# Early-fusion megakernel: last layernorm in token rows, softmax row sums on GpSimd, new order on every engine

## The reference, cut to what matters

```
h = concat(tokens(x) * pos, txt)
h = h + retention(layernorm(h))                  # A: 8 heads, complex, per-head norm, gate
u = layernorm(h)
q, k, v = u @ Wq + bq, u @ Wk + bk, u @ Wv + bv  # B: 8 heads of 16
attn = softmax(q k^T / 4)                        # rows of 97
o = (attn @ v) @ Wo + bo
t = layernorm(u + o) * ln1_g + ln1_b             # C
probs = softmax(t @ gate_W + gate_b)
out = h + expert[argmax](t) * max(probs)         # gelu((t @ W1) + b1) @ W2 + b2
```

## Time and profile before

| | |
|---|---|
| median of 3 runs | 1401.92 us (1400.88 to 1402.66) |
| the profiled execution, its own time | 1397.03 us |
| its span | 1395.2 us |
| PE busy, share of the span | 1346.4 us, 96% |
| DVE busy | 1008.2 us, 72% |
| ACT busy | 718.4 us, 51% |
| POOL busy | 407.4 us, 29% |
| mean granted TensorE clock | 0.993 |
| chain that ended last, share of PE | 90% |

### The profile page before, as it was taken

One profiled execution on the slowest core, in us unless ns is written; L12 is line 12 of the kernel. 1 busy time (PEld: TensorE's weight loads), 2 busy tenths in 40 slices (PEclk: granted clock), 3 DMA queues, 4 the chain that ended last, 5 costly groups with the idle time before them and its releaser, 6 DMA issues.

```text
span 1395.2 us, 40349 instructions
## 1 busy us (share of the span) xinstructions
PE 1346.4 (96%) x14878; PEld 988.3 (71%) x14879; DVE 1008.2 (72%) x2331; ACT 718.4 (51%) x1630; POOL 407.4 (29%) x268
## 2 busy tenths in 40 slices
PE   7899999999999999999999999999999986999998
PEld 5566666666666666666666666666666554999998
DVE  2677777777777777777777777777777865666665
ACT  2255555555555555555555555555555554556555
POOL 0002222222222222222222222222222225655666
PEclk9999999999999999999999999999999998999999
DMA  9422322232222222322222222232331002343332
GB/s 388 141 73 77 84 85 84 84 84 85 84 85 84 85 85 84 85 83 84 85 80 78 78 83 84 85 85 85 85 85 40 14 14 54 93 125 106 103 101 67
DMA packets 95130, 124.61 MB, mean 89 GB/s; under 512 B 56619, under 2 KB 77149, under 8 KB 94592
## 3 DMA queue, kind: packets, MB, share of 16 engines
q1 hardware_dynamic: 38400, 102.47, 22.9%
q0 software_dynamic: 56576, 19.93, 6.8%
HBM read 101.27 MB, written 20.82 MB: 88 GB/s over the span
## 4 chain that ended last, share of the span: by engine, by line
PE 90%; DVE 3%; issue 2%; DMA 2%; POOL 1%; ACT 1%; SPq 0%; DVEq 0%; POOLq 0%; ACTq 0%
PE bank_emb L427 19%; PE bank_z L415 9%; PE bank_s L486 8%; PE bank_y L500 6%; PE bank_s L725 5%; PE bank_s L415 5%; PE bank_x L415 5%; PE bank_s L552 4%; PE bank_x L592 4%; PE bank_y L415 3%; PE bank_z L574 3%; PE bank_x L714 3%; PE bank_y L714 3%; PE bank_x L564 2%; PE bank_s L536 2%
## 5 line engine op out<-in xcount | busy, mean ns | idle before, releaser
L1448 POOL DMA_INDIRECT expert_rows<-row_sb,placei x128 | 276.4, 2159 | 320.7 <-issue 320.7
L427 PE MATMUL bank_emb<-home_x 128*128 128x256 f32 (+1 forms) x1216 | 339.6, 390 | 6.8 <-DMA home_x<-in_x_main 6.8
L427 PEld LDWEIGHTS bank_emb<-home_x 128*128 128x128 f32 (+1 forms) x1216 | 218.2, 191 | 109.8 <-issue 37.7
L1021 DVE TENSOR_TENSOR home_s<-bank_s,con 97x776 f32<-97x776 f32 x256 | 239.7, 957 | 1.8
L1434 POOL COPY h<-txt 128x128 f32<-128x128 f32 x32 | 9.4, 294 | 589.7 <-DVE h L1071 566.0
L1035 DVE TENSOR_REDUCE mx<-bank_s 97x8 f32<-97x776 f32 x128 | 117.7, 961 | 48.8 <-PE bank_s L552 48.8
L1460 POOL DMA_INDIRECT out_tokens<-yo,tok x104 | 121.4, 1168 | 75.5 <-issue 64.2
L486 PE MATMUL bank_s<-qm,xn 32*97 32x452 f32 x1024 | 131.5, 577 | 2.1 <-DVE home_s L1040 1.2
L869 ACT ACTIVATE home_s<-home_s 97x776 f32<-97x776 f32 x128 | 107.8, 842 | 28.6 <-DVE home_s L1040 28.5
L1040 DVE TENSOR_TENSOR home_s<-bank_s,mx 97x776 f32<-97x776 f32 x128 | 117.2, 956 | 0.0
L725 PE MATMUL bank_s<-w2e,home_s 128*128 x832 | 110.1, 276 | 0.0
(11 more groups left out here) (211 smaller groups left out, 2381.2 us busy)
## 6 DMA issues: line engine op xcount, KB each, us to landing
home_x<-in_x_main SPq DMA_DIRECT2D x96, 768.0 KB, 4.5
home_x<-expert_rows SPq DMA_DIRECT2D x104, 129.0 KB
w1e<-in_exp_w SPq DMA_DIRECT2D x1, 2576.0 KB, 11.7
txt<-in_txt_t SPq DMA_DIRECT2D x32, 64.0 KB
w2e<-in_exp_w SPq DMA_DIRECT2D x1, 2048.0 KB, 17.6
expert_rows<-row_sb,placei POOLq DMA_INDIRECT x128, 7.3
out_tokens<-yo,tok POOLq DMA_INDIRECT x104
home_x<-in_x_tail SPq DMA_DIRECT2D x32, 48.0 KB
```

Source lines behind the costliest of these rows:

```text
L427: mm = pe.matmul(banks["emb"][:, 0:NPG], wtok[0:k, c, :], x_sb[0:k, c, :], start=(c == 0), stop=(c == KC - 1))
L1021: ins = dve.tensor_tensor(sm[:, k % 2, 2 * h:2 * h + 2, :], pair(h), decay, ALU.mult)
L1448: pool.indirect_dma_start(out=rows[:, :], out_offset=bass.IndirectOffsetOnAxis(ap=placei[:, k, c:c + 1], axis=0), in_=row_sb[:, k, c, E:E ...
```

## The change

The layernorm at the end of B is no longer made in the layout of features on partitions. `c_rows` multiplies z itself by `gate_rows`, whose gate columns now hold `gate_W * ln1_g`; the squares, their sum, the logarithm, the exponential and the scaling are done on the token rows (97 partitions, 4 x 136 elements, and 97x4 for the statistics); `ln1_g` and `ln1_b` are applied in the expert stage when a transposed tile is copied out of PSUM, and `gate_bias` takes in `ln1_b @ gate_W`. The row sums of B's softmax are added up by POOL in a tree of eight additions for each half group, DVE takes their reciprocals, each repeated 16 times, into `rexp` (97x512), PE transposes that in four pieces, and ACT copies the result. Every engine's order and the bank table are new, and the rounds end one earlier (`LAST`).

```diff
-    ("B.scores1.0", "s0 s1", 2), ("B.scores1.1", "s2 s3", 2), ("A.var", "z", 0), ("C.var2", "z", 3),
+    ("A.scores3.0", "s0 s1", 1), ("A.scores3.1", "s2 s3", 1), ("B.hrows", "z", 2), ("B.probs_t0.2", "s3", 2),
...
-FIRST, LAST = -2, NG + 4
+FIRST, LAST = -2, NG + 3
...
+SUM_ORDER = [(1, 2), (0, 1)]
...
-        rsb = sb("rsb", [P, N])
+        rsb = sqb
...
# PE
+            pe.matmul(s2[0:S, 2 * P:2 * P + E], const("ones")[:, 0:S], gate_wb[:], start=True, stop=True).then_inc(s_mm, 1)
...
-            def b_sums(g, k):
-                ps = use(g, "B.den") if k == 0 else banks[BANK_OF["B.den"]]
...
+            def b_sums(g):
+                pe.wait_ge(s_rden, g + 1)
+                ps = use(g, "B.den")
+                for c in range(G):
+                    mm = pe.transpose(ps[:, c * S:(c + 1) * S], rexp[:, c, :], const("ident")[0:S, 0:S])
+                done(mm, "B.den")
...
-            def c_var(g):
-                pe.wait_ge(s_sqc, g + 1)
-                product(g, "C.var2", const("mean"), sqc[:])
...
-                pe.wait_ge(s_th, g + 1)
+                read(pe, g, "B.wo")
...
-                    mm = pe.matmul(ps[0:S, c * (E + P):(c + 1) * (E + P)], th[:, t:t + S], gate_rows[:],
+                    mm = pe.matmul(ps[0:S, c * (E + P):(c + 1) * (E + P)], z2[:, t:t + S], gate_rows[:],
...
# ACT
-                act.activation(sqc[:], z2[:], ACT.Square).then_inc(s_sqc, 1)
+                act.activation(sqc[:], row_sb[:, g % ROWS, :, E:E + P], ACT.Square).then_inc(s_sqc, 1)
...
-                log(g, "C.var2", rsc[:])
+                act.wait_ge(s_vsum, g + 1)
+                act.activation(rsc[:], vsum[:], ACT.Ln, bias=const("eps", S), scale=1.0 / P).then_inc(s_logc, 1)
...
-                drain(act.activation(rden[:], ps[:, 0:N], ACT.Ln), "B.den")
-
-            def sums_reciprocal(g):
-                read(act, g, "B.den")
-                act.activation(rden[:], rden[:], ACT.Exp, scale=-1.0).then_inc(s_rden, 1)
+                drain(act.copy(rden[:], ps[:, 0:N]), "B.den")
...
# DVE
+            def sums_reciprocal(g):
+                for k in range(2):
+                    dve.wait_ge(s_sum, SUMMED[g, k])
+                if g:
+                    full(dve, g - 1, "B.den")
+                dve.reciprocal(rexp[:].rearrange("p c (q d) -> p (c q) d", d=DH),
+                               rsum[:].rearrange("p c r o -> p (c r o)").unsqueeze(2).to_broadcast(
+                                   [S, G * H, DH])).then_inc(s_rden, 1)
...
-            def c_normal(g):
+            def c_sum(g):
+                dve.wait_ge(s_sqc, g + 1)
+                dve.tensor_reduce(vsum[:], sqc[:], AX.X, ALU.add).then_inc(s_vsum, 1)
+
+            def c_scale(g):
                 dve.wait_ge(s_rsc, g + 1)
...
-            def c_affine(g):
...
+                r = row_sb[:, g % ROWS, :, 0:E + P]
+                dve.tensor_tensor(r, r, rsc[:].unsqueeze(2).to_broadcast([S, G, E + P]), ALU.mult).then_inc(s_scaled, 1)
...
-                dve.tensor_copy(t_t[:, s, :], banks[bank_t[s % 2]][:, 0:P]).then_inc(s_in, 1)
+                dve.tensor_scalar(t_t[:, s, :], banks[bank_t[s % 2]][:, 0:P], column("ln1_g"), column("ln1_b"),
+                                  ALU.mult, ALU.add).then_inc(s_in, 1)
...
# POOL
+            def b_sum(g, k):
+                for h in range(2):
+                    pool.wait_ge(s_prob, PROB[g, k, h])
...
+                p = prob[:, k, :, :].rearrange("p r (j t) -> p (r j) t", t=S)
+                first = 5 * (SUMMED[g, k] - 1)
+                pool.tensor_tensor(tree[:], p[:, :, 0:48], p[:, :, 48:96], ALU.add).then_inc(s_tree, 1)
+                for step, n in enumerate((24, 12, 6, 3)):
+                    pool.wait_ge(s_tree, first + step + 1)
+                    pool.tensor_tensor(tree[:, :, 0:n], tree[:, :, 0:n], tree[:, :, n:2 * n], ALU.add).then_inc(s_tree, 1)
+                pool.wait_ge(s_tree, first + 5)
+                pool.tensor_tensor(tree[:, :, 3], tree[:, :, 0], tree[:, :, 1], ALU.add)
+                pool.tensor_tensor(tree[:, :, 4], tree[:, :, 2], p[:, :, S - 1], ALU.add).then_inc(s_tail, 1)
...
-                at(scatter, i - 4)
+                at(b_sum, i - 2, 1)
                 at(text, i + 1)
+                at(scatter, i - 3)
+                at(b_sum, i - 1, 0)
```

More of the change, by code:

```diff
@@ L220, in fusion @@
         pt = sb("pt", [S, 2, 4, 4 * S])
+        tree = sb("tree", [S, 16, 48])
+        rsum = sb("rsum", [S, G, 4, 2])
+        rexp = sb("rexp", [S, G, P])
         rden = sb("rden", [P, N])
@@ L647, in _ @@
             for i in range(FIRST, LAST):
-                at(ahead, i + 1, 2, 3)
-                at(b_scores, i - 2, 1)
-                at(ahead, i + 1, 3, 4)
-                at(a_var, i)
+                at(a_mix, i - 1, 1)
+                at(a_mix, i - 1, 2)
+                at(a_scores, i - 1, 3)
+                at(b_hrows, i - 2)
                 at(ahead, i + 1, 4, 6)
-                at(c_var, i - 3)
-                at(ahead, i + 1, 6, 8)
-                at(a_gate, i - 1)
-                at(a_scores, i - 1, 3)
@@ L693, in _ @@
-                at(a_mix, i, 1)
                 at(b_mix, i - 2, 0)
                 at(b_mix, i - 2, 1)
+                at(ahead, i + 1, 15, 17)
+                at(b_sums, i - 2)
+                at(ahead, i + 1, 17, 19)
+                at(a_scores, i, 1)
+                at(a_mix, i, 0)
+                at(a_center, i + 1)
+                at(b_values, i - 1)
                 at(a_scores, i, 2)
+                at(a_var, i + 1)
+                at(ahead, i + 2, 0, 3)
                 at(b_wo, i - 2)
-                at(b_probs_t, i - 1, 0, 2)
@@ L1441, in scatter @@
                 pool.sem_inc(s_turn, 1)
-                for half in range(2):
-                    read(pool, g, f"C.rows{half}")
-                    pool.sem_inc(s_turn, 1)
                 read(pool, g, "B.hrows")
```

255 lines of the change are left out of this document (127 added, 128 removed), and 18 rows, old and new, of the table USES.

## The result

The changed kernel takes 1481.83 us, median of 4 runs (1474.02 to 1485.55), beside 1401.4 us for the kernel before (1400.47 to 1402.66, 4 runs): a ratio of 1.0568 (1.0531 to 1.0605), slower by 5.7%, outside the range and on the other side. Its profiled span is 1483.7 us, 88.5 more than before, with a mean granted clock of 0.959 (0.993 before); the medians lie 80.4 us apart, since the profiled execution of the kernel before (1397.03 us) is shorter than its four runs, and that of the changed kernel (1485.55) is the longest of its four.

The account below looks back on a forecast made before the run. PE alone was taken to bound the middle: 33.47 less 1.73 plus 0.65 of lateness gives a 32.4 us round. Thirty rounds save 32 us, the tail 3: 1401.92 - 35 = 1367 us, range 1342 to 1412.

Parts of the forecast that it names:

- the price of the reciprocal: 97x512 reciprocal on DVE: taken as 0.72 us, the low bound, with a high bound of 5.1 us.
- Rival A: Reciprocal between b_key and next b_max takes several steps an element: 5.1 us, time 1490; chance 0.20 beyond 2.6 us.
- Rival B: POOL and DVE hold each other up at gate_one and c_scale: 1.2 us a hold, time 1397 to 1403; chance 0.12.
- PE's 1.73 us a round: On PE, c_var's 0.73 and b_sums' 1.34 go, four transposes' 0.34 come: 1.73 us less a round.
- The 1.0 net for the sums: On PE, the b_sums products' 1.34 us go and four rexp transposes at 0.34 us come.
- The round: Distance between the same DVE step, 568.95 us taken as 17 rounds: 33.47 us before, 32.4 after.
- Step (3): From first b_scores to second a_scores, PE has 3.56 us, DVE's maxima and shifts take 0.1 + 3.67: 0.2 late.
- (1) to (4): Four PE stretches against DVE: 0.05, 0.2 and 0.2 us late, the fourth in time; 0.65 a round with 0.2 for sharing.
- The tail: Chain behind z loses a product and two ACT steps of 388 columns, gains small ones: 3 us saved.
- The expert stage: 104 tiles; the copy out of PSUM becomes a same-size multiply and add on the same engine: nothing.
- The tree: POOL's eight additions for each half group: 5.8 us, between bounds of 3.5 and 9.3; costs nothing of itself.
- the transposes: Four PE transposes of rexp, taken at 0.34 us like an existing row of four.

Follow-up runs that it names:

- e3_narrow_few: Changed kernel with a 97x32 reciprocal repeated by ACT, and GpSimd adding only three keys' columns and a one; 0.9913 of the kernel before, round 33.97 us.
- e2_few_keys: Changed kernel, wide reciprocal kept, with GpSimd adding only three keys' columns and a one instead of all 97; 1.0598 of the kernel before, round 37.36 us.
- e10_old_order_narrow: e8_rows_only plus used trees, 97x32 reciprocal, and four transposes in place of the sums' 16 products; 0.9894 of the kernel before, round 34.75 us.
- e1_narrow: Changed kernel with a reciprocal of 97x32 instead of 97x512, repeated by ACT; 1398.99 us, 1.0138 of the kernel before.
- e11_old_order_wide: e10_old_order_narrow with the change's 97x512 reciprocal, so all of the change but its engine order; 1.0673 of the kernel before, mean round 38.05 us.
- e15_new_order_again: e3_narrow_few unchanged, on a chip of the 1401 us kind; 0.9837 of the kernel before, round 34.22 us.
- e6_narrow_late: e1_narrow with the second tree of a round held back until one_hot is done; 1.0177 of the kernel before, round 35.17 us.
- e8_rows_only: Kernel before with only the last layernorm in token rows, old engine order, sums still products; 0.9886 of the kernel before, round 33.96 us.

## Why the prediction was wrong, point by point

**The step that failed is the price of the reciprocal.** The forecast took "0.72, since the fixed parts of the operations in the earlier trace rows differ by more (141 for the sum, 166 for the cast) than the 10 ns in question". It measures 3.34. With 180 ns for 4 elements, 342 for 32 and 3342 for 512, an element costs 162 / 28 = 5.8 and 3000 / 480 = 6.25 ns, six times that of the sum; the repeated reading of one value adds nothing to speak of. The fixed part is then 142 to 157 ns, between the two that the forecast had named, and some 25 of the 180 ns were the slope. A range of 1.06 to 9.75 ns an element, with both ends from rows, should not have been settled by the end that suits the forecast; 0.72 us against a cover of 0.25 left everything to this number. The Trainium skill, page VectorE: DVE Perf Modes, section Walkthrough: the 8-slice pipeline in each mode, gives reciprocal a repeat count of 8, from which the forecast had worked out an estimate of 4.3 us. The trace agrees that it is an operation of several steps an element; its 3.34 us are 22% below that estimate. Rival A should have had the larger chance. But with 3.34 us in it the forecast's own sum gives a round of 34.8 and a time of 1438 us, still 44 too few: the clock, the sums and the tail below are terms that it had at nothing or with the wrong sign.

**Rival A is what happened**, with its place (between `b_key` and `b_max`) and its wait (`a_scores` on `b_shift`). Its size came out by another sum. Its rule was: what lies over 0.25 us of cover goes straight onto the round. By that the 2.62 us over the forecast make PE wait 2.37; it waits 1.74, so there was more cover. The other half of the price is the clock: from e3_narrow_few to e2_few_keys, on one chip and with one order, 3.39 us are 1.81 of waiting and 1.58 of a lower clock behind it. No step of the forecast had a price for that.

**Rival B happened too.** `c_scale` 1.35 for 0.71 and `logits` 0.87 for 0.19 are what it described. They are worth 0.95 us a round with the narrow reciprocal and about as much with the wide one at equal clock; only the mean of e2_few_keys hides it. The Trainium skill, page SBUF — State Buffer, section Who interferes with whom, has DVE share one of its port pairs with GpSimd under an exclusive lock. The runs agree on whom it meets: operations with two inputs in SBUF beside a tree (L1098, L1113, L1073), while operations with one, beside the same trees, keep their length. In e10_old_order_narrow (`y_normal` with one input in PSUM, `y_gated` with two in SBUF, `c_sum` with one):

```profile
532.41 0.62 DVE L1070 SCALAR_TENSOR_TENSOR yn<-bank_y,col,rsy 128x388 f32<-128x388 f32 x1
533.07 1.34 DVE L1076 SCALAR_TENSOR_TENSOR yn<-yn,col,gate 128x388 f32<-128x388 f32 x1
534.53 0.67 DVE L1101 TENSOR_REDUCE vsum<-sqc 97x4 f32<-97x512 f32 x1
536.13 0.72 DVE L1106 TENSOR_TENSOR row_sb<-row_sb,rsc 97x544 f32<-97x544 f32 x1
```

```profile
532.99 2.69 POOL L1466 TENSOR_TENSOR tree<-tree 97x384 f32<-97x384 f32 x4
536.25 0.70 POOL L1471 TENSOR_TENSOR rsum<-tree 97x16 f32<-97x16 f32 x1
```

The tree runs beside all four (531.07 to 536.95). `y_gated` starts 0.08 us behind an addition and is held; `c_scale` starts 0.12 us ahead of the last addition and keeps its length, and the addition takes 0.70 us where it takes 0.24 alone. So the hold goes both ways, against the one that starts later.

**PE's 1.73 us a round.** The 0.73 for `c_var` is right (0.75, twice). The 1.0 net for the sums is not (its 16 products are those of both halves; the time was read for both, so the count did no harm): it took the distance between two starts as the price of a step wherever it stands. Measured are 0.05 in the old order and nothing in the new one on the chip of the 1379 us kind, where other PE steps were dearer by as much.

**The round.** 568.95 us are 16 rounds. Since the sum went by differences, this changed neither time nor range, but it understated the round by 2 us. It hid nothing else: DVE's share, 76% before and 82% after, was read from busy time.

**What is late next.** Step (3), `b_scores` to `a_scores`, was the right place. The 0.65 us for (1) to (4) and sharing cannot be read apart. In e1_narrow PE waits 0.27 us a round on `a_query_imag` and 0.20 on `gate_times`, neither of them among the four.

**The tail.** Minus 3 us was forecast, plus 24 measured. Beside 101.5 us of the kernel before (last two distances and the way to the expert stage; 101.9 on the other kind of chip), the layernorm in rows alone costs 3.6 to 4.8, the trees alone 7, both in the old order with the narrow reciprocal 11.6 (113.1 us), the whole change 24 (125.2). Where chains set the pace, each link counts: the trees and the chain of square, sum, logarithm, exponential, scaling and logits are longer than what they replace. The last 12 are the wide reciprocal: e11_old_order_wide, which has it in the old order, already takes 124.8 us. How much of them is waiting and how much clock was not tried apart.

**The expert stage** at nothing was right (1.8 us with the end of the program). The tree (5.8 for 5.66), the transposes (0.34 for 0.33) and `c_sum` were right as well.

In parts, as ratios to the kernel before on chips of the 1401 us kind: the layernorm in rows 0.986; with the sums by GpSimd and a narrow reciprocal 0.989; with the wide one 1.067; with the new order 1.057. The new order softens the wide reciprocal by one point. With the narrow one it is slower than the old: 1.014 on the other kind of chip, which the difference between e3_narrow_few and e15_new_order_again makes an estimated 1.006 here.

## What to carry to other kernels

An operation whose price per element no row shows must be measured, or carried at its dear end, when it stands on the way between two uses of a bank with a quarter of a us of cover; do such an operation on the few distinct values (97x32, 0.34 us) and repeat them afterwards, on an engine with room. Where PE is full, a new gap of 1 to 2 us can cost nearly twice its length, so compare single rounds with their granted clock and not only the mean. Work given to GpSimd should be set against every DVE operation beside it that reads two inputs from SBUF, since the hold moves to the next such operation when the tree is moved (e6_narrow_late). On an engine that is full, a step is worth what the round loses without it, not the distance to the next start: try the removal alone, one part at a time, which here would also have found the fastest kernel that computes the whole result, e8_rows_only.
